# A four-layer conditioned stack on one core: Wx loaded in quarters, the last period's second layer four steps earlier, and y's low part on GpSimd

## The reference

```python
# 0: a wavelet transform scaled and put together again; it comes to x + x*gate
h = silu(cond @ W1.T + b1); gate = sigmoid(h @ W2.T + b2)
# 1: a recurrence over the 512 tokens, h0 = cond
h = tanh(x_t @ Wx + b + h @ Wh)
# 2: f = sigmoid(x @ Wf.T + bf); i = sigmoid(x @ Wi.T + bi); c = x @ Wh.T + bh
s = f + i + EPS; info = (i / s) * c; keep = f / s + EPS
P = cumprod(keep, tokens); scaling[t] = product of keep from t on
out = cumsum(scaling * info) + P * cond
# 3: a layer with weights made from cond, rank 8
ae = layernorm(cond) * g + b; w = gelu(ae @ w1 + b1) @ w2 + b2   # split into A and B
out = x + x @ (base + A @ B.T)
```

## Time and profile before

| what | us |
|---|---|
| median of 3 runs | 1487.49 (1482.9 to 1489.01) |
| the profiled execution, its own time | 1487.07 |
| its span, first to last instruction | 1485.0 |
| front, to the first step | 0 to 37 |
| recurrence, 16 periods of about 73.4 | 37 to 1210 |
| block 15 through the second layer, first batch | 1210 to about 1293 |
| batches 1 to 15 and the last stores | to 1485 |

### The profile page before, as it was taken

One profiled execution on the slowest core, in us unless ns is written; L12 is line 12 of the kernel. 1 busy time (PEld: TensorE's weight loads), 2 busy tenths in 40 slices (PEclk: granted clock), 3 DMA queues, 4 the chain that ended last, 5 costly groups with the idle time before them and its releaser, 6 DMA issues.

```text
span 1485.0 us, 49924 instructions
## 1 busy us (share of the span) xinstructions
PE 1423.4 (96%) x21159; PEld 1122.8 (76%) x21159; DVE 1005.8 (68%) x2707; ACT 659.5 (44%) x2184; POOL 684.8 (46%) x538
## 2 busy tenths in 40 slices
PE   6889999999999999999999999999998996899998
PEld 4558888888888888888888788888886775677776
DVE  4344757575767676767676766666656689899995
ACT  4445454545454544454444444444444442233333
POOL 2432444444444343435353535353524346777774
PEclk9899999999999999999999999999998898999999
DMA  9760333333333333333333333332315447889993
GB/s 345 264 231 6 52 66 52 65 52 66 54 64 58 60 59 59 59 59 59 59 60 61 61 60 60 59 64 54 58 32 106 115 105 130 273 308 333 332 329 140
DMA packets 441904, 168.15 MB, mean 113 GB/s; under 512 B 406433, under 2 KB 409633, under 8 KB 438354
## 3 DMA queue, kind: packets, MB, share of 16 engines
q1 hardware_dynamic: 441296, 164.79, 43.9%
q10 hardware_dynamic: 386, 0.18, 0.0%
HBM read 96.78 MB, written 68.16 MB: 111 GB/s over the span
## 4 chain that ended last, share of the span: by engine, by line
PE 80%; DVE 10%; issue 7%; ACT 1%; POOL 1%; DMA 0%; ACTq 0%; DVEq 0%; POOLq 0%
PE bank L466 48%; PE recb L432 28%; DVE aux L1200 4%; DVE scanS L1192 2%; PE bank L626 2%; DVE xt L1203 1%; PE bank L517 1%; DVE pre L1158 1%; DVE pre L1156 1%; DVE hs L1163 0%; DMA xa<-in_ln_b 0%; DVE pout L1222 0%; ACT hs L651 0%; ACT konst L652 0%; POOL xt L896 0%
## 5 line engine op out<-in xcount | busy, mean ns | idle before, releaser
L432 PEld LDWEIGHTS recb<-hs,scanS 128*128 128x128 f16 x16384 | 443.9, 96 | 174.4 <-DVE hs L1163 172.4
L432 PE MATMUL recb<-hs,scanS 128*128 128x32 f16 x16384 | 495.1, 177 | 24.3 <-DVE hs L1163 23.7
L651 ACT ACTIVATE hs<-pre 128x64 f16<-128x64 f32 x512 | 131.7, 257 | 623.9 <-DVE pre L1158 623.1
L1156 DVE TENSOR_TENSOR pre<-recb,xw 128x64 f32<-128x64 f32 x512 | 115.0, 225 | 264.6 <-PE recb L432 260.7
L1022 DVE RECIPROCAL gates<-gates 128x64 f32<-128x64 f32 (+1 forms) x484 | 258.2, 554 | 0.4
L1163 DVE TENSOR_TENSOR hs<-konst,hs 128x64 f16<-128x64 f32 x512 | 115.1, 225 | 137.1 <-ACT konst L652 137.1
L881 POOL TENSOR_TENSOR xt<-xt,hbuf 128x512 f32<-128x512 f32 (+1 forms) x65 | 98.9, 1522 | 178.6 <-ACT hbuf L655 178.6
L869 POOL TENSOR_TENSOR x1lo<-xt,x1hi 128x512 fp32r<-128x512 f32 x64 | 82.1, 1284 | 190.8 <-ACT x1hi L661 190.8
L887 POOL TENSOR_TENSOR gates<-gates 128x512 f32<-128x512 f32 x64 | 82.9, 1296 | 167.0 <-DVE gates L1022 167.0
L896 POOL TENSOR_TENSOR xt<-xt,pout 128x512 f32<-128x512 f32 x64 | 75.8, 1185 | 151.2 <-DVE pout L1048 146.1
L1158 DVE TENSOR_TENSOR pre<-recb,pre 128x64 f32<-128x64 f32 x512 | 114.9, 224 | 17.6
(11 more groups left out here) (214 smaller groups left out, 2740.2 us busy)
## 6 DMA issues: line engine op xcount, KB each, us to landing
xt<-in_x SPq DMA_DIRECT2D x64, 256.0 KB, 3.5
g_d<-gst SPq DMA_DIRECT2D x64, 256.0 KB, 3.8
n_d<-nst SPq DMA_DIRECT2D x64, 256.0 KB, 3.0
x_d<-xt SPq DMA_DIRECT2D x64, 256.0 KB, 3.1
out<-gates SPq DMA_DIRECT2D x64, 256.0 KB, 6.5
xt<-x_d SPq DMA_DIRECT2D x28, 512.0 KB, 4.8
stage<-in_w SPq DMA_DIRECT2D x11, 1024.0 KB, 7.1
xt<-g_d SPq DMA_DIRECT2D x14, 512.0 KB, 6.9
```

Of the source, the lines that this page charges most:

```text
L432: last = nc.tensor.matmul(rec[:, m].rearrange("p a b -> p (a b)"), w[:, k, m * P:(m + 1) * P], hs[:, k].rearrange("p a b -> p (a b)"), sta ...
L651: nc.scalar.activation(hs[:, :, 0, :], pre[t % 2][:], ACT.Tanh, scale=unscale).then_inc(s_h, 1)
L1156: nc.vector.tensor_tensor(pre0[:], rec[:, :, 0, :], xw[j % 2][:, t], ALU.add).then_inc(s_pre0, 1)
```

## The change

- **Front.** Wx comes in four transfers of a chunk each, alternating with those of x, with a semaphore each. cond has its own semaphore, so that LayerNorm's sum waits for cond alone and not for the two LayerNorm rows. Square and what follows it stand ahead of the gate's sigmoid and product. TensorE makes all high parts of Wx first, then the low ones; the transposes and dense layers between them move behind low chunks 0 to 2.
- **Last period.** `moved_up` makes tables for j = 15 in which the second layer's items come AHEAD = 4 steps earlier, and items that were carried past the end of the period come into its steps 28 to 31. TensorE's groups of block 14 go to steps 4 to 27. The queues after the recurrence lose what is thereby done: reciprocal pieces, new info 2 and 3, a seed copy and half a decay, the last forget share. x2's low parts there are all four VectorE's (two were GpSimd's). `decays`, two halves with seeds in PSUM, takes the place of `whole_decay`.
- **Factors.** The low part of A is a ScalarE copy (it was VectorE's), that of B is GpSimd's (it was VectorE's).
- **y's low part.** ScalarE copies y once more, whole, into SBUF (`yf`), and GpSimd makes y's low part from it, behind `x3_low` of the next batch's second chunk. The batch's last products and the next batch's first factor product wait for these.

The core of the diff:

```diff
@@ -45,6 +45,28 @@
             29: [("s", 3)], 30: [("r", 3, 1), ("r", 3, 2)], 31: [("r", 3, 4), ("r", 3, 5)]}
+AHEAD = 4
+def moved_up(table, kinds):
+    out = {}
+    for t, items in table.items():
+        for item in items:
+            if t < CARRIED:
+                out.setdefault(t, []).append((t, item))
+            if item[0] not in kinds and t >= CARRIED:
+                out.setdefault(t, []).append((t, item))
+            elif item[0] in kinds:
+                at = (t if t >= CARRIED else t + TS) - AHEAD
+                if at < TS:
+                    out.setdefault(at, []).append((at + AHEAD, item))
+    return out
+ACT_LAST = moved_up(ACT_WORK, "fig")
+DVE_EARLY_LAST, DVE_LATE_LAST = (moved_up(t, ("x1", "s", "r", "n", "p", "k")) for t in (DVE_EARLY, DVE_LATE))
@@ -256,7 +279,7 @@
                 load_x(0, m)
-            sp.dma_start(wx, a["Wx"]).then_inc(d_wx, 16)
+                sp.dma_start(wx[:, m, :], a["Wx"][:, m, :]).then_inc(d_wx[m], 16)
             sp.dma_start(wh, a["Wh"]).then_inc(d_wh, 16)
@@ -454,15 +477,16 @@
                         pe.wait_ge(s_x1l, C * (b + 1))
-                    else:
-                        pe.wait_ge(s_x2h, C * (b + 1))
-                        pe.wait_ge(s_x2l, C * (b + 1))
-                        if b == 0:
-                            pe.wait_ge(s_w3l, 3 * C)
+                    elif b == 0:
+                        pe.wait_ge(s_w3l, 3 * C)
                 whi, wlo = split[kind]
...
                     k, (w, act) = e // 3, ((whi, ahi), (wlo, ahi), (whi, alo))[e % 3]
+                    if n == C and e % 3 == 0:
+                        pe.wait_ge(s_x2h, C * b + k + 1)
+                    elif n == C and e % 3 == 2:
+                        pe.wait_ge(s_x2l, C * b + k + 1)
                     last = nc.tensor.matmul(bank[n % C][:], w[:, k, m * P:(m + 1) * P], act[:, k, :], start=(e == 0), stop=(e == GM - 1))
@@ -509,24 +533,25 @@
             last.then_inc(s_cols, 1)
-            for k in range(C):
-                pe.wait_ge(s_x1h, k + 1)
-                for e, w in enumerate(split["x"]):
+            for e, w in enumerate(split["x"]):
+                for k in range(C):
+                    pe.wait_ge(s_x1h, k + 1)
                     pe.wait_ge((s_wxh, s_wxl)[e], k + 1)
...
                         nc.tensor.matmul(bank[m][:], w[:, k, m * P:(m + 1) * P], x1hi[:, k, :], start=(k == 0 and e == 0), stop=False)
-                if k == 1:
-                    pe.wait_ge(s_mx, 1)
-                    pe.wait_ge(s_turned, 2)
-                    nc.tensor.transpose(peak, whs[:, 0:1], ident[:]).then_inc(s_amx, 1)
-                elif k == 2:
-                    pe.wait_ge(s_wh, 5)
-                    nc.tensor.matmul(spread, ones[:], whr[:, 0:4], start=True, stop=True).then_inc(s_bc, 1)
-                    pe.wait_ge(s_colsT, 1)
-                    pe.wait_ge(d_h1, 16)
-                    dense(aeT, w1h, 2, z3)
-            pe.wait_ge(d_wh, 16)
-            dense(condT, wh, None, z)
+                    if e and k == 0:
+                        pe.wait_ge(s_mx, 1)
+                        pe.wait_ge(s_turned, 2)
+                        nc.tensor.transpose(peak, whs[:, 0:1], ident[:]).then_inc(s_amx, 1)
+                    elif e and k == 1:
+                        pe.wait_ge(s_colsT, 1)
+                        pe.wait_ge(d_h1, 16)
+                        dense(aeT, w1h, 2, z3)
+                        pe.wait_ge(s_wh, 5)
+                        nc.tensor.matmul(spread, ones[:], whr[:, 0:4], start=True, stop=True).then_inc(s_bc, 1)
+                    elif e and k == 2:
+                        pe.wait_ge(d_wh, 16)
+                        dense(condT, wh, None, z)
             pe.wait_ge(s_x1l, C)
@@ -549,9 +574,12 @@
                     step(j, t)
-                    for n, lo in ((e // GM, e % GM) for e in range(t * QUOTA, (t + 1) * QUOTA)):
-                        if GROUPS[n][0] != "x" or j + 1 < NBLK:
-                            group_part(n, lo, lo + 1, j)
+                    if j + 1 < NBLK:
+                        for e in range(t * QUOTA, (t + 1) * QUOTA):
+                            group_part(e // GM, e % GM, e % GM + 1, j)
+                    else:
+                        for e in range(max(C * GM, (t + AHEAD) * QUOTA), min(len(GROUPS) * GM, (t + AHEAD + 1) * QUOTA)):
+                            group_part(e // GM, e % GM, e % GM + 1, j)
                     if j == NBLK - 1 and t == 2:
@@ -576,10 +604,8 @@
                 for k in range(C):
-                    if n == 0 and k < C // 2:
-                        pe.wait_ge(s_x2l, C * b + k + 1)
-                    elif n == 0:
-                        pe.wait_ge(s_lowd, k - C // 2 + 1)
+                    if n == 0:
+                        pe.wait_ge(s_lowd, k + 1)
                     last = nc.tensor.matmul(bank[n % C][:], split[kind][0][:, k, m * P:(m + 1) * P], x2lo[:, k, :], start=False, stop=(k == C - 1))
@@ -706,24 +732,25 @@
             nc.scalar.dma_start(row[:], a["rows"]).then_inc(d_rows, 16)
-            nc.scalar.dma_start(crow, a["cond"]).then_inc(d_ln, 16)
+            nc.scalar.dma_start(crow, a["cond"]).then_inc(d_crow, 16)
             for dst, k in ((lng, "ln_g"), (lnb, "ln_b")):
...
             nc.scalar.dma_start(bias4[:], a["bias"]).then_inc(d_bias, 16)
+            act.wait_ge(s_ln, 2)
+            nc.scalar.activation(ae[:], cent[:], ACT.Square, accum_out=stat[:, 1:2]).then_inc(s_ln, 1)
             act.wait_ge(s_z, 1)
             nc.scalar.activation(sg[:], z, ACT.Sigmoid).then_inc(s_sg, 1)
-            act.wait_ge(s_ln, 2)
-            nc.scalar.activation(ae[:], cent[:], ACT.Square, accum_out=stat[:, 1:2]).then_inc(s_ln, 1)
             act.wait_ge(s_ln, 4)
...
             nc.scalar.activation(sg[:], z, ACT.Sigmoid).then_inc(s_sg, 1)
-            act.wait_ge(d_wx, 16)
+            act.wait_ge(d_wx[0], 16)
             nc.scalar.copy(split["x"][0][:, 0, :], wx[:, 0, :]).then_inc(s_wxh, 1)
...
                 if m + 1 < C:
+                    act.wait_ge(d_wx[m + 1], 16)
                     nc.scalar.copy(split["x"][0][:, m + 1, :], wx[:, m + 1, :]).then_inc(s_wxh, 1)
@@ -747,7 +774,8 @@
                     tanh(j, t)
-                    for kind, m in ACT_WORK.get(t, []):
+                    plan = [(t, item) for item in ACT_WORK.get(t, [])] if j + 1 < NBLK else ACT_LAST.get(t, [])
+                    for at, (kind, m) in plan:
                         if kind == "x1h":
@@ -811,6 +841,9 @@
                 nc.scalar.copy(ysh[b % 2], yp[b % 2]).then_inc(s_yh, 1)
+                if b >= 2:
+                    act.wait_ge(s_yl, b - 1)
+                nc.scalar.copy(yf[b % 2], yp[b % 2]).then_inc(s_yf, 1)
@@ -821,7 +854,6 @@
                 x2_high(last, m)
-            forget_share(last - 1, 3)
             for n in range(4):
@@ -948,11 +977,29 @@
                 add_P(j - 1, 0)
-                if j + 1 < NBLK:
-                    add_h(j, 3)
-                else:
-                    add_h(j, 3, 0, OCT - 2)
-                    add_h(j, 3, OCT - 2, OCT)
+                add_h(j, 3)
+            def base_low(m):
+                pool.wait_ge(s_bh, m + 1)
+                nc.gpsimd.tensor_tensor(blo[:, m, :], braw[:, m, :], bhi[:, m, :].bitcast(F32), ALU.subtract).then_inc(s_bl, 1)
+            j = NBLK - 1
+            add_h(j, 0)
+            pool.wait_ge(s_xbh, 1)
+            nc.gpsimd.tensor_tensor(xbl.bitcast(F32R), xbraw, xbh, ALU.subtract).then_inc(s_xbl, 1)
+            shares(j - 1, 0)
+            base_low(0)
+            add_h(j, 1)
+            shares(j - 1, 1)
+            base_low(1)
+            base_low(2)
+            shares(j - 1, 2)
+            add_h(j, 2)
+            add_P(j - 1, 0)
+            base_low(3)
+            shares(j - 1, 3)
+            add_h(j, 3, 0, OCT - 2)
+            add_h(j, 3, OCT - 2, OCT)
@@ -965,13 +1012,15 @@
+            def y_low(b):
+                pool.wait_ge(s_yh, b + 1)
+                pool.wait_ge(s_yf, b + 1)
+                nc.gpsimd.tensor_tensor(ysl[b % 2], yf[b % 2], ysh[b % 2].bitcast(F32), ALU.subtract).then_inc(s_yl, 1)
             last = NBLK - 1
-            for m in range(C // 2):
-                x2_low(last, m)
-            shares(last - 1, 3)
             add_P(last - 1, 1)
+            add_P(last - 1, 2)
             shares(last, 0)
-            add_P(last - 1, 2)
             add_P(last - 1, 3)
@@ -991,14 +1040,20 @@
             x3_low(C)
+            y_low(0)
             times_n(C + 3)
...
                 x3_low(k - 3)
+                if (k - 3) % C == 1:
+                    y_low((k - 3) // C - 1)
             for k in range(SLOTS - 3, SLOTS):
                 x3_low(k)
+                if k % C == 1:
+                    y_low(k // C - 1)
+            y_low(B - 1)
@@ -1091,19 +1146,20 @@
             nc.vector.memset(aeT[:], 0.0)
-            dve.wait_ge(d_ln, 48)
+            dve.wait_ge(d_crow, 16)
```

(46 more changed lines are left out.)

45 lines of the change are left out of this document (18 added, 27 removed).

## The result

The changed kernel takes 1480.89 us (median of 20 runs, 1473.81 to 1483.35), the kernel before beside it 1487.78 (1482.69 to 1489.23): ratio 0.9953, 95% interval 0.9942 to 0.9964. That is inside the bound of 0.5% that the prediction set, by a hair, and 0.6 us above the predicted 1480.3. The profiled execution took 1480.85 us, with a span of 1479.1.

A forecast was written before the change was run, and what follows sets the result against it. TensorE was taken to bound most of the span, VectorE the stretch after the recurrence and the batches. The terms summed as 1487.07 + 0.4 − 4.0 − 3.15 = 1480.3 us, range 1475.5 to 1486.

The forecast's parts named there:

- Part 1: Front: a table load of 1.28 us behind Square moves the gate's product from 10.61 to 11.03; 0.4 us lost.
- Rival F: Front: the switch of table costs a drain as well, 1.4 us more, giving 1481.7; chance 0.03.
- the cover that the prediction named: Front: x's high part waits for the gate and not for Wx, so finer Wx transfers give nothing.
- Part 2: Last period and after: moved work costs the recurrence 0; batch 0 through VectorE 4.5 us sooner, 4.0 reaching batch 1.
- rival E: Recurrence: moved work meets full steps, 24 steps grow by 0.3 us and eat all gain, 1487; chance 0.03.
- the half clock: Last groups after the recurrence: ten matmuls at 1.2 GHz, 0.43 instead of 0.23 us each, costing 2.1 us.
- the walk: Step-by-step timing after the recurrence: gate sums at 1220.45, 1226.6, 1234.9 and 1243.25, batch 0 through VectorE 4.5 us sooner.
- Part 3: Batches: without y's low part VectorE needs 12.18 us, TensorE sets the pace at 13.06; 3.15 us gained.
- the ring: Steady batches: the loop of waits through GpSimd takes 12.7 us, 0.35 below TensorE's 13.06.
- B: Rival: more is gained, by no table load or a clock rising sooner or never falling; 1476.5 to 1479, chance 0.24.
- C: Rival: new waits through GpSimd take part back; 1483.5, or 1485.5 with a clock slow to rise; chance 0.16.
- D: Rival, batches: late loads of x make each batch pay; slower needs 13.6 us a batch; chance 0.04.

The follow-up runs named there:

- e3: Changed kernel with spare matmuls in the last period's light steps and behind the last one; group medians 1472.8 us (2 runs) and 1478.3 us (4 runs).
- e4: Changed kernel with y's low part of batch 0 ahead of one product and one x low part in GpSimd's queue; ratio 0.9953 to the kernel before.
- f1: Changed kernel with whole decay scans, seeds in SBUF, instead of pairs of half scans seeded from PSUM; ratio 0.9981 to the kernel before.
- f2: Changed kernel with y's low part made three times on GpSimd, twice for nobody; ratio 1.0002 to the kernel before.
- e1: Kernel before with only y's low part moved to GpSimd, from a ScalarE copy; median 1480.13 us, ratio 0.9963 to the kernel before.

## Why the prediction was right

**What bounds, and the sum.** The reading by stretch held: 1480.3 forecast, 1480.89 measured, and the two terms that carry it, 4.0 and 3.15, came out at 3.49 and 3.22. That the sum agrees to 0.6 us is in part luck. In the profiled pair the front lost 0.4 more and the stretch behind the recurrence gained 0.5 less than forecast. Two things that the sum didn't have cancel: the slower pace of the second and third period cost 0.7, and the shorter last period gave 0.8. Execution time beyond the span was 0.3 less. And the median stands near 1481.0 since 14 of the 20 runs fell in the upper group; with most in the lower one it would have been near 1476.5, still inside the range.

**Part 1.** The mechanism held: Square as ScalarE's first function brings a load of 1.28 us ahead of the sigmoid. The loss was 0.8 instead of 0.4 in the profiled execution. The mis-sized term is cond's landing, 6.0 for 5.5; four other executions of the same front (the runs e3, e4, f1 and f2 of the table) put the gate's product at 10.78 to 11.21 (forecast 11.03), so over the five this term jitters by 0.7 us, and their mean, 11.13, is 0.5 behind the old front's 10.61 and 10.73 (e1), as forecast. By the first state nothing of it can be told: it comes at 37.06 to 38.62 in the five and at 37.81 and 38.10 with the old front, since TensorE's work between the first x matmul and the first step takes 17.8 us in some of these traces (17.9 and 18.0 with the old front) and 16.9 in others. What the prediction didn't see is that the loss was avoidable: the gate could have come at 9.5. The rule of the Trainium skill that a switch of table costs 2.66 us (ScalarE: Activation LUTs, What ACT_TABLE_LOAD costs) doesn't hold here: the sigmoid starts 0.01 us behind the end of the load. Rival F falls. That the order high parts first gives nothing agrees with the traces (17.78 us from the first x matmul to the first step for 17.88); for Wx's split it is argued, by the cover that the prediction named.

**Part 2.** That the moved work costs the recurrence nothing held: its last period is even 0.76 us shorter, with its slow step at 3.47 for 3.63, no second slow step (2.67 before) and a second light stretch at its end, so rival E falls. "What is late next is TensorE" held. The term that was mis-sized is the half clock: twelve matmuls, from 1212.57 to 1217.82, went at it where the walk had ten, the first gate sum stood 11.00 us after the last state where the walk had 10.27, and keeping the clock up gives 2.45, not 2.1. The later gate sums stood 0.5 to 0.8 behind the walk by it. From the last state on, batch 0 was through VectorE 4.05 us sooner (the last add at 1263.72 for 1267.00, and the last states at 1210.95 and 1210.18) where 4.5 was forecast. Decay pairs of 2.0 us stand in the place of 3.1, and f1 shows that they carry 3.8 us.

**Part 3.** The period of 13.05 us (13.06 forecast), the ring of 12.66 (12.7), the low part of 0.45 (0.4) and TensorE's wait for it in batch 0 all held. Batch 0's low part was there at 1273.97 (1272.5 forecast), TensorE's last chunk products about 2.6 us ahead of it. Half a microsecond was to be lost between VectorE and batch 1's first copy out; 4.05 − 3.49 = 0.56 was, and by the cause named: behind batch 0's copies out GpSimd runs without a pause from 1277.44, ten operations (the walk had nine) and then the low part of batch 1 at 1289.88. VectorE, busy 18.1 of the 18.9 us from 1270.82 to 1289.67, stands close behind as a bound: with GpSimd's queue ahead (e4) it lets batch 1 come only 0.8 sooner.

**The rivals.** B didn't happen, but the run with TensorE kept busy bears out its price: a clock that doesn't fall is 2.4 us. C needed a ring above 13.06, and has 12.66. D: no load ends a wait of over 0.7 us in the steady batch looked at. What moves a run by 5 us was in none of the cases: the pace of the recurrence. The range of 1475.5 to 1486 covers it only since it was wide for other reasons.

## What to carry to other kernels

Steps in which TensorE has little to do cost nothing here by themselves, but they can cost the clock behind them: whoever makes a stage ready sooner or moves work out of it should look at the granted clock of the stretch that gets lighter and of the one behind it, and can hold it with spare matmuls into a bank that nobody reads (2.4 us here). Beside busy GpSimd give VectorE's scans one operand in PSUM (two halves in 2.0 us for 3.1), and put the first user of a ScalarE table where no load stands between it and the critical path. When work moves to another engine's in-order queue, place its first instance by hand: the steady place can be late in the first batch (2.8 us at batch 0's copies out here, of which 0.8 reached batch 1).
